# Two indirect transfers in flight: GpSimd waits on even and odd semaphores ahead of each scatter and gather

## What is computed

```
x: (4, 512, 128) float32           # 2048 tokens = 16 tiles of 128
layer 0: xattn (8 heads of 64)     ffn: 8 experts, hidden 512, best 1 expert for each token
layer 1: xattn (16 heads of 8)     ffn: 16 experts, hidden 256, best 3 experts, weighted by their gates
layer 2: xattn (16 heads of 8)     ffn: ternary weights and a low-rank part
layer 3: xattn (16 heads of 8)     ffn: each token picks a tile of a small spline network
```

## Time and profile before

| | us |
|---|---|
| median of 3 runs (613.02 to 614.86) | 614.35 |
| the profiled execution | 612.8 |
| its span in the trace | 610.9 |
| busy in the span: PE, DVE, ACT, POOL | 448.9, 346.2, 229.4, 212.8 |

### The profile page before, as it was taken

The page is one execution under the profiler, slowest core; times in us unless marked ns, Lnnn a source line. Parts: engine busy times, 40 slices in busy tenths (PEclk is TensorE's granted clock), DMA queues, the critical chain, the costliest instruction groups (busy, mean ns, idle before and its releaser), DMA issues.

```text
span 610.9 us, 9548 instructions
## 1 busy us (share of the span) xinstructions
PE 448.9 (73%) x2682; PEld 365.7 (60%) x2682; DVE 346.2 (57%) x1230; ACT 229.4 (38%) x596; POOL 212.8 (35%) x269
## 2 busy tenths in 40 slices
PE   3877772899878876931799646836969999996950
PEld 2765572698846665531599645815757676783840
DVE  3645365564567765317344223456686758867885
ACT  1111000465544641110366333514355656654420
POOL 5100165002441156766100524546621225552014
PEclk9895555899998995555899967877779999996555
DMA  7389992222192000111233433211100000000002
GB/s 207 72 311 355 383 408 104 60 64 64 53 294 91 0 28 30 53 47 39 82 107 104 121 84 100 69 44 39 32 1 1 2 0 1 2 2 1 1 2 69
DMA packets 59256, 53.82 MB, mean 88 GB/s; under 512 B 11618, under 2 KB 45491, under 8 KB 59076
## 3 DMA queue, kind: packets, MB, share of 16 engines
q1 hardware_dynamic: 52996, 43.76, 22.4%
q0 software_dynamic: 4096, 8.40, 4.9%
q10 hardware_dynamic: 2112, 1.05, 0.6%
HBM read 24.35 MB, written 28.84 MB: 87 GB/s over the span
## 4 chain that ended last, share of the span: by engine, by line
PE 47%; DVE 17%; issue 9%; ACT 8%; another core or an unknown queue 6%; DVEq 4%; POOL 4%; DMA 2%; SPq 1%; ACTq 0%; POOLq 0%
PE bank L1953 8%; PE bank L1964 7%; PE bank L1840 5%; PE bank L1856 4%; PE bank L1845 3%; ACT xn L1454 3%; PE bank L1976 2%; POOL rowbuf L535 2%; PE bank L1828 2%; ACT r L1537 1%; DVE stats L652 1%; PE bank L1871 1%; PE bank L1688 1%; DVE x L1130 1%
## 5 line engine op out<-in xcount | busy, mean ns | idle before, releaser
L535 POOL DMA_INDIRECT rowbuf<-h_sb,slots x64 | 63.0, 984 | 35.4 <-DVE slots L937 17.8
L522 POOL TENSOR_SCALAR nmr<-mv 128x4 f32<-128x4 f32 x32 | 7.8, 245 | 171.1 <-DVE veps L659 161.5
L1537 ACT ACTIVATE r<-bank,b 128x128 f32<-128x128 f32 x224 | 64.5, 380 | 4.6 <-PE bank L1964 4.0
L1964 PE MATMUL bank<-wall,r 128*128 x448 | 62.4, 286 | 2.6 <-DVE h_sb L1144 2.1
L546 POOL DMA_INDIRECT vZ<-rowbuf,slots x40 | 38.6, 966 | 71.7 <-DMA rowbuf<-h_sb 60.8
L1144 DVE TENSOR_TENSOR h_sb<-bank,b2all 128x128 f32<-128x128 f32 x88 | 22.5, 286 | 69.9 <-PE bank L1976 35.0
L1964 PEld LDWEIGHTS bank<-wall,r 128*128 128x128 f32 x448 | 57.5, 201 | 3.0 <-issue 3.0
L1856 PE MATMUL bank<-vB,eT 128*128 128x36 f32 x384 | 50.6, 281 | 1.9 <-ACT eT L1473 1.9
L1856 PEld LDWEIGHTS bank<-vB,eT 128*128 128x128 f32 x384 | 50.7, 206 | 2.0 <-ACT eT L1473 2.0
L1953 PE MATMUL bank<-on,eT 128*128 128x128 f32 x224 | 32.4, 290 | 22.7 <-ACT r L1537 17.2
L1840 PE MATMUL bank<-VW,xnT_all 128*128 128x512 f32 x64 | 40.5, 725 | 10.4 <-ACT xnT_all L1462 6.6
(11 more groups left out here) (272 smaller groups left out, 919.5 us busy)
## 6 DMA issues: line engine op xcount, KB each, us to landing
rowbuf<-zero SPq DMA_DIRECT2D x17, 1024.0 KB, 11.5
wall<-in_w SPq DMA_DIRECT2D x4, 2048.0 KB
h_sb<-rowbuf SPq DMA_DIRECT2D x88, 64.0 KB
rowbuf<-h_sb SPq DMA_DIRECT2D x88, 64.0 KB
x<-in_x ACTq DMA_DIRECT2D x4, 256.0 KB, 5.2
rowbuf<-h_sb,slots POOLq DMA_INDIRECT x64
b2all<-in_L_ffn_b SPq DMA_DIRECT2D x1, 1024.0 KB, 16.6
out<-h_sb SPq DMA_DIRECT2D x4, 256.0 KB, 2.6
```

The source lines that it names most:

```text
L535: nc.gpsimd.indirect_dma_start(rowbuf[0:MOE[l][0] * REGION * P], bass.IndirectOffsetOnAxis(slots[:, k * T + t:k * T + t + 1], 0), tile_of( ...
L1537: i = a.activation(mid_rows(l, p * R + j, c), mid_bank(l, p * R + j, c), ACT.Relu, bias=b1[l][:, bass.ds(e[j] * C + c, 1)])
L1964: i = mm(second_bank(l, s), mid_rows(l, s, c), wall[:, bass.ds(e[j] * n + (WHALF + c * P), P)], start=(c == 0), stop=(c == C - 1))
```

## The change

Ahead of each scatter but the first two of a mixture, and ahead of each gather but the first two of a batch, GpSimd waits until the last but one transfer of that kind has landed. To make that wait exact, transfers count in turn on two semaphores, one for even and one for odd numbers. VectorE and SyncE wait for both where they waited for one. No transfer, size or order is changed. Between one batch's gathers and the next one's, and between scatters and gathers, nothing new is waited for.

```
@@ semaphores
-        s_sc_x = sem("s_sc_x")
+        s_sc_x = [sem(f"s_sc_x{i}") for i in range(2)]
-        s_gat = [sem(f"s_gat{b}") for b in range(B)]
+        s_gat = [[sem(f"s_gat{b}_{i}") for i in range(2)] for b in range(B)]
-        gather_before = {1: 0, 3: 16 * T * TOPK[1]}
-        landed = {1: 16 * W * TOPK[1], 3: 16 * W * (TOPK[1] + TOPK[3])}
+        gather_before = {1: 0, 3: 8 * T * TOPK[1]}
+        landed = {1: 8 * W * TOPK[1], 3: 8 * W * (TOPK[1] + TOPK[3])}
@@ SyncE, ahead of the first tile loads
-                sp.wait_ge(s_sc_x, gather_before[l] + 16 * T * TOPK[l])
+                for i in range(2):
+                    sp.wait_ge(s_sc_x[i], gather_before[l] + 8 * T * TOPK[l])
@@ scatter
                         t = b * W + w
-                        nc.gpsimd.indirect_dma_start(...).then_inc(s_sc_x, 16)
+                        n = t * TOPK[l] + k
+                        if n >= 2:
+                            pool.wait_ge(s_sc_x[n % 2], gather_before[l] + 16 * (n // 2))
+                        nc.gpsimd.indirect_dma_start(...).then_inc(s_sc_x[n % 2], 16)
@@ gather
                 for i in range(first, last):
                     c = i % K * T + b * W + i // K
-                    nc.gpsimd.indirect_dma_start(...).then_inc(s_gat[b], 16)
+                    if i >= 2:
+                        pool.wait_ge(s_gat[b][i % 2], landed[l] - 8 * W * K + 16 * (i // 2))
+                    nc.gpsimd.indirect_dma_start(...).then_inc(s_gat[b][i % 2], 16)
@@ VectorE, add_experts (and the same in beside for l = 3)
-                dve.wait_ge(s_gat[b], landed[l])
+                for i in range(2):
+                    dve.wait_ge(s_gat[b][i], landed[l])
```

More of the change, by code:

```diff
@@ L534, in scatter @@
                         t = b * W + w
-                        nc.gpsimd.indirect_dma_start(rowbuf[0:MOE[l][0] * REGION * P], bass.IndirectOffsetOnAxis(slots[:, k * T + t:k * T + t + 1], 0), tile_of(xn_all, t), None).then_inc(s_sc_x, 16)
+                        n = t * TOPK[l] + k
+                        if n >= 2:
+                            pool.wait_ge(s_sc_x[n % 2], gather_before[l] + 16 * (n // 2))
+                        nc.gpsimd.indirect_dma_start(rowbuf[0:MOE[l][0] * REGION * P], bass.IndirectOffsetOnAxis(slots[:, k * T + t:k * T + t + 1], 0), tile_of(xn_all, t), None).then_inc(s_sc_x[n % 2], 16)
             def gather(l, b, first, last):
@@ L545, in gather @@
                     c = i % K * T + b * W + i // K
-                    nc.gpsimd.indirect_dma_start(tile_of(yg[l][b], i), None, rowbuf[0:MOE[l][0] * REGION * P], bass.IndirectOffsetOnAxis(slots[:, c:c + 1], 0)).then_inc(s_gat[b], 16)
+                    if i >= 2:
+                        pool.wait_ge(s_gat[b][i % 2], landed[l] - 8 * W * K + 16 * (i // 2))
+                    nc.gpsimd.indirect_dma_start(tile_of(yg[l][b], i), None, rowbuf[0:MOE[l][0] * REGION * P], bass.IndirectOffsetOnAxis(slots[:, c:c + 1], 0)).then_inc(s_gat[b][i % 2], 16)
             def add_bo(b):
@@ L1201, in beside @@
                         if s == at:
-                            dve.wait_ge(s_gat[b], landed[3])
+                            for i in range(2):
+                                dve.wait_ge(s_gat[b][i], landed[3])
                         if at <= s < at + 3:
```

## The result

| | kernel before | changed kernel |
|---|---|---|
| median of 20 runs, us | 615.73 (611.19 to 622.78) | 610.40 (602.74 to 617.24) |
| profiled execution, us (span) | 612.8 (610.9) | 607.06 (605.2) |
| mean granted clock of the profiled execution | 0.800 | 0.792 |

The ratio, after over before, is 0.986, 95% interval 0.982 to 0.989: 1.4% faster, where I had forecast 0.7% slower. The time lies inside the range of 609 to 624, the sign is wrong.

The account below looks back on a forecast made before the run. The prediction took the chain of waits, half TensorE, to bound the kernel, GpSimd mostly waiting. Terms 3.9 + 0.1 + 0.4 + 0 gave 4.4 us on a median of 614.35: 618.7 us, with 609 to 624 for 8 in 10.

Parts of the forecast that it names:

- Part 1: Scatters of l = 1 under DMA load: late landings delay scatter 3, norm 7 and the first mixture matmul, +3.9 us.
- The Trainium skill's rule: Nearly constant 2.0 us plus bytes over 436 GB/s: 64 KB transfers land in 2.15 us, so the change costs nothing.
- Part 2: Scatters of l = 3: landing of 2.23 us just within the 2.25 limit, +0.1 us, ends 0 and +1.0.
- the 5.17 us before the last 12: Spare time in l = 3 of the 36 earlier scatters, which end ahead of the last row numbers.
- Part 3: Gathers: landing over the limit slows the pace from 1.25 to 1.34 us, +0.4 us, ends +0.2 and +0.8.
- my upper bound of 1.44: Slowest pace forecast for gathers, in us each, from a landing of 2.6 us and a restart of 0.27.
- Part 4: TensorE signals held during transfer trains: unchanged at pace 1.34, so 0 taken; unknown from about -12 to +5 us.
- The count of 1.42 us: In gather and scatter trains, each transfer occupies something for 1.42 us while GpSimd issues one each 1.25.
- Rival B: Gathers of both mixtures: thinner trains let TensorE's signals through; 606.2 us with half gone, 610.4 with a third; chance 0.25.
- picture of a pile: In transfer trains, transfers issued faster than 1.42 us pile up, and TensorE's signal stands back until the pile is gone.
- A: No difference: norm 7's delay in l = 1 is not passed on or is taken up later; 614.7 us, chance 0.14.
- C: Slower still: held signals last as long as the longer gather trains, about 4.5 us more; 623.2 us, chance 0.12.

Follow-up runs that it names:

- b3: Waits ahead of scatters alone, gathers free, against the kernel before on a chip with held signals (near 621 us): ratio 1.007.
- c1: Changed kernel with the four scatters ahead of norm 7 in l = 1 freed from waits, against the kernel before (near 621 us): ratio 0.978, three runs.
- a4: No scatter waits, each gather waits for the one just before, against the kernel before (585 to 590 us, no held signals): ratio 1.127.
- a2: Waits ahead of gathers alone, scatters free, against the kernel before on a chip without held signals (585 to 590 us): ratio 1.011.
- b1: The kernel before, unedited, run again against itself on a chip with held signals (near 621 us): ratio 1.003.
- c2: No scatter waits, each gather waits for the last but two (three in flight), against the kernel before (near 621 us): ratio 0.994, four runs.
- c3: No waits on landings; GpSimd clears 320 unused columns ahead of gathers, 1.49 us apart, against the kernel before (near 621 us): ratio 0.984.
- b4: Waits ahead of gathers alone, scatters free, against the kernel before on a chip with held signals (near 621 us): ratio 0.991.
- a1: Waits ahead of scatters alone, gathers free, against the kernel before on a chip without held signals (585 to 590 us): ratio 1.017.
- a3: No waits on landings; one unused column cleared between gathers, pace still 1.25 us, against the kernel before (585 to 590 us): ratio 1.004.
- c4: Waits on the gathers of l = 3 alone, against the kernel before on a chip with held signals (near 621 us): ratio 0.988.

## Why the prediction was wrong

**Part 1, right.** Forecast: scatter 2 and 3 late, norm 7 and the first matmul +3.9 us. Measured: +4.2 and +4.4. The landings came as forecast (84.85 and 86.22 against 84.8 and 86.2); the extra comes from the start of scatter 2 0.77 us after the landing instead of 0.27, with scatter 3 right behind it. As a time of its own the loss is near the 0.7% of b3, and c1 took it back. One cover went: the last scatter of l = 1 started at 110.25 (forecast 106) and landed after the tile list instead of before it, so SyncE's first tile load is 5.5 us late (107.20 to 112.73), of which the first matmul shows 4.4. The Trainium skill's rule that I set against this part ("DMA: Bandwidth & Descriptors", section "Anatomy of one DMA — SWDGE (gpsimd) path") would have had scatter 0 land before scatter 2's turn; the trace disagrees, with 4.42 us of idle time.

**Part 2, about right on the path, for other reasons.** The train of l = 3 scatters grew from 73.0 to 73.6 us between its first and its last start: +0.6 where I took +0.1 with +1.0 as the end. But the 5.17 us before the last 12 are gone, and the train is chain from 246.37 on. Those 5.17 us were themselves the work of a held signal, VectorE's wait of 8.05 us. Without it the last row numbers are there at 275.1 instead of 277.4, although all ahead of them is 4 us late. One landing of 4.05 us and the scatters with two waits, which start 0.77 us after a landing, then used up what that gave.

**Part 3, the size is where it began to go wrong.** The restart of 0.27 us that I took from the earlier trace rows is right for a gather, which has one wait ahead of it (0.26 in a4 and a2). The landing is what I had too short. I took 2.4 us, 2.3 to 2.6, out of the 2.66 us of the earlier trace rows; as GpSimd sees it, the median is 2.57 in a4 and 2.67 in a2, which gives 1.42 to 1.47 us a gather, around my upper bound of 1.44. In the changed kernel's first train a pair took 2.97 us (346.58 to 349.55), which is 1.49 a gather and by the restart of 0.26 a landing of 2.71, and the next pair, with a slower landing, took 4.11 (349.55 to 353.66); the mean was 1.58 a gather. Nothing in my sum stood for the slow landings. On the path the six gathers behind norm 17 took 1.6 us longer from first to last start (8.03 against 6.40), where I had +0.4.

**Part 4, the step that failed: "held signals, 0 taken".** It hung on one comparison: at a pace below 1.42 us nothing changes, above it nothing piles up. With 1.34 from part 3 I stood on the wrong side, and a term taken as 0 was a gain of some 11.8 us in the stretch of the gathers. The count of 1.42 us holds up: the held copies end 17.3 us after the first of 12 gathers in b1 (343.37 to 360.64) and c2 (346.67 to 363.96), 1.44 each. Rival B had the mechanism. That the median is B's 610.4 us for a third of the 25.1 us is luck: VectorE's waits fell by 7.5 us (30%), but the sum behind it is 11.8 us won in the gathers against 5.7 lost ahead of them and 0.4 behind, from a kernel before whose median is 615.73 and not 614.35. What B had against it, "two in flight is what the gathers had already, since 2.5 us hold two of them", was the same error as in part 3: a landing mostly takes more than 2.5 us, so holding the third gather back for it spaces the trains. c3 shows that this spacing, set without any wait on a landing, brings the gain.

**What the picture of a pile does not explain.** At 1.49 us, above 1.42, c3 still has held signals up to 5.1 us, so the limit isn't sharp. Nor do VectorE's waits rank the variants: c1 has 18.0 us of them and the lowest ratio. That the gain of the gather waits needs held signals is shown: 0.991 (0.986 to 0.996) where traces have them (b4), 1.011 (0.999 to 1.022) where they don't (a2). What holds a signal, why only on some chips, and whether the pace or the two in flight counts, stays open.

Rivals A and C are out: A by norm 7's row, C since the first train of gathers grew from 13.8 to 17.4 us between its first and twelfth start while its longest held signal shrank from 12.15 to 4.42 us.

## What to carry to other kernels

An engine's wait marked "remote" that ends with a train of another engine's transfers is a price on that train's pace: slow the train a little (here from 1.25 to 1.5 us a gather), by whatever is at hand, and keep the throttle off transfers that stand ahead of work on the chain, as the four scatters ahead of norm 7. Work out the pace that a throttle sets with the landing as the waiting engine sees it, not as another engine's start suggests, and count the waits that stand ahead of the transfer: a second one cost 0.5 us here. Where the outcome flips at a number within a tenth of your estimate, give both sides nearly equal chances. Time it on more than one chip: the change won 1.3 to 1.4% on two, while its two parts cost 1.7% and 1.1% on one without held signals, where the whole change wasn't run.

## What the runs showed of the hardware

- Chips differ by 5 to 6% for this kernel (585 to 590 against 620 to 622 us). The traces show where most of it is: 28.8 us of remote waits on VectorE against none, and 92 us (b1) against 68 (a1, a3) from the first to the last gather of l = 3, at the same pace of 1.25 us.
- GpSimd starts an indirect transfer 0.26 to 0.27 us after the landing that releases it when that wait stands alone (a4, a2, and 252.07 in the changed kernel), as after VectorE's signal, and 0.77 us after it when a wait on row numbers stands there too (85.62). One gather each of b4 and c4 took 0.86. Back to back, 0.30 us lie between two transfers.
- An indirect transfer of 128 rows of 512 bytes landed 2.23 us after its start as a scatter and after 2.57 us in the median as a gather (a4). With the DMA engines full (share 1.05 at that place) scatter 0 of the changed kernel took 6.1 us, 78.72 to 84.85.
- Of GpSimd's 0.30 us between two indirect transfers 0.11 us of other work is free; 0.38 us of it makes 1.49 us of 1.25.
